# Opening of an expert loop: rows of the first tiles loaded by another engine, first turned rows kept and first gate products in another order

## The reference

```python
x = hidden_states.reshape(-1, D)                       # 4096 tokens, D = 256
scores = softmax(x @ gate_w.T)                         # E = 64 experts
topk_w, topk_idx = top_k(scores, TOP_K)                # 6 experts for each token
buf[se, pos_c] = x[st]                                 # tokens sorted by expert
g = einsum('ecd,efd->ecf', buf, w_gate)                # F = 176
u = einsum('ecd,efd->ecf', buf, w_up)
eo = einsum('ecf,edf->ecd', silu(g) * u, w_down)
y = zeros_like(x).at[st].add(eo[se, pos_c] * weights)
```

## Time and profile before

| | us |
|---|---|
| median of 3 runs | 1659.45 |
| lowest and highest | 1658.81, 1660.39 |
| the profiled execution, own time | 1659.82 |
| its span in the trace | 1658.0 |

### The profile page before, as it was taken

How to read it: one execution, slowest core, us unless ns; L and a number is a source line. 1 busy time by engine, 2 the same in 40 slices (tenths; PEclk the granted TensorE clock), 3 DMA queues, 4 the chain that set the end, 5 groups by cost and what they waited for, 6 DMA issues and landing times. The chain is left out here.

```text
span 1658.0 us, 44404 instructions
## 1 busy us (share of the span) xinstructions
PE 1496.2 (90%) x12590; PEld 1005.8 (61%) x12655; DVE 1272.3 (77%) x4402; ACT 1003.2 (61%) x2284; POOL 786.5 (47%) x848
## 2 busy tenths in 40 slices
PE   7995889999999999999974499999999999997997
PEld 4664667677777777777763255555555555554775
DVE  4663777888888888889884587777777777773887
ACT  4773676767667776676661266666666666662221
POOL 1333233666666666666677334433433443442333
PEclk9996899999999999999995699999999999998999
DMA  3874454554555542223223666666666667524996
GB/s 115 258 236 154 128 156 124 158 160 150 156 160 160 159 148 89 88 82 94 92 69 108 175 183 203 195 194 199 201 192 195 205 191 204 183 79 97 251 246 144
DMA packets 264982, 264.40 MB, mean 159 GB/s; under 512 B 87467, under 2 KB 236313, under 8 KB 264752
## 3 DMA queue, kind: packets, MB, share of 16 engines
q1 hardware_dynamic: 203504, 175.70, 36.8%
q0 software_dynamic: 19968, 51.16, 8.5%
q10 hardware_dynamic: 41280, 34.77, 8.3%
HBM read 142.70 MB, written 122.98 MB: 160 GB/s over the span
## 5 line engine op out<-in xcount | busy, mean ns | idle before, releaser
L1745 POOL DMA_INDIRECT scratch_y<-e_eo,e_goes x224 | 222.6, 994 | 357.8 <-ACT e_eo L1828 314.4
L1770 PE MATMUL e_psGU<-wexp,e_xT 128*64 x896 | 290.1, 467 | 0.0
L1772 PE MATMUL e_psGU<-e_up,e_xT 128*64 128x352 f32 x896 | 290.0, 467 | 0.0
L1374 POOL TENSOR_TENSOR f_wnr<-f_wss,f_half 128x4 f32<-128x4 f32 x96 | 112.2, 1169 | 197.0 <-DVE f_wss L1197 196.9
L1364 POOL DMA_INDIRECT scratch_buf<-rows,dest x180 | 183.2, 1018 | 44.9 <-issue 43.5
L1849 ACT ACTIVATE e_up<-wexp 128x704 f32 x224 | 176.9, 790 | 20.6 <-POOLq L1735 20.6
L1770 PEld LDWEIGHTS e_psGU<-wexp,e_xT 128*64 128x64 f32 x896 | 113.8, 137 | 121.8 <-issue 121.8
L1964 DVE COPY e_down<-wexp 128x512 f32 x224 | 94.1, 420 | 101.2 <-PE e_psD L1793 99.2
L1828 ACT ACTIVATE e_eo<-e_psD 128x256 f32<-128x256 f32 x224 | 85.7, 385 | 93.7 <-PE e_psD L1793 47.0
L1817 ACT ACTIVATE e_sgm<-e_psGU 128x176 f32<-128x176 f32 x224 | 71.2, 318 | 93.3 <-PE e_psGU L1772 92.1
L1787 PE MATMUL e_psD<-wexp,e_hT 112*64 x448 | 115.2, 378 | 1.6 <-DVE e_hT L1925 1.6
(11 more groups left out here) (332 smaller groups left out, 4365.2 us busy)
## 6 DMA issues: line engine op xcount, KB each, us to landing
e_xg<-scratch_buf ACTq DMA_DIRECT2D x448, 66.0 KB
scratch_y<-f_blank SPq DMA_DIRECT2D x64, 384.0 KB
c_g<-scratch_y SPq DMA_DIRECT2D x64, 384.0 KB, 5.8
scratch_qkvT<-q_tT SPq DMA_DIRECT2D x16, 768.0 KB
wexp<-in_wgT SPq DMA_DIRECT2D x64, 176.0 KB
wexp<-in_wuT SPq DMA_DIRECT2D x64, 176.0 KB
scratch_buf<-f_blank SPq DMA_DIRECT2D x65, 132.0 KB, 1.9
scratch_kv<-q_y SPq DMA_DIRECT2D x16, 512.0 KB, 2.8
```

Of the source, the lines that this page charges most:

```text
L1374: pool.tensor_tensor(wnr[:, x, cols], wss[:, x, cols], half[:, 0:Q], ALU.pow).then_inc(wn1[x].sem, 1)
L1745: pool.indirect_dma_start(out=T["y"], out_offset=bass.IndirectOffsetOnAxis(goes[:, n:n + 1], 0), in_=eo[:, n % OB, :], in_offset=None, bou ...
L1770: pe.matmul(psGU[0:RT, n % 2, 0:2 * F], xT[:, n % 4, k, 0:RT], ring[:, bass.ds(at[n] + k * 2 * F, 2 * F)], start=(k == 0), stop=(k == KD - 1))
L1772: mm = pe.matmul(psGU[RT:P, n % 2, 0:2 * F], xT[:, n % 4, k, RT:P], up2[:, n % 2, k * 2 * F:(k + 1) * 2 * F], start=(k == 0), stop=(k == K ...
```

## The change

SyncE issues the twelve loads of tiles 2 to 7 at the start of the phase, ahead of its wait for tiles 0 and 1, and ScalarE no longer does. ScalarE makes the keeps of tiles 0 and 1 between the two first copies of up matrices, and those of tiles 2 and 3 right behind. TensorE makes the gate products of tile 0 ahead of the turns of tiles 2 and 3, and those of tile 1 behind them. From tile 2's gate products on all is as before.

```diff
--- before.py
+++ after.py
@@ -1699,6 +1699,10 @@
         @block.sync
         def _(sp):
             sp.sem_inc(ready, FIRST)
+            for m in range(2, GB, 2):
+                for i, starts in numbers(mybir.EngineType.SP, first_row, 0, E * STRETCH, m).items():
+                    for h, at in enumerate(starts):
+                        sp.dma_start(xg[i][h * RT:(h + 1) * RT, :], T["buf"][bass.ds(at, RT), :]).then_inc(gi[i], 16)
             for m in range(2):
                 sp.wait_ge(gi[m], 32)
             for ex in range(FIRST, NB):
@@ -1798,7 +1802,16 @@
                     if 0 <= m < NT:
                         stage(m)
 
-            for n in range(-4, NT + 2, 2):
+            each(turn_x, 0)
+            find(0)
+            gate_up(0)
+            each(turn_x, 2)
+            find(2)
+            gate_up(1)
+            each(turn_x, 4)
+            find(4)
+            each(turn_h, 0)
+            for n in range(2, NT + 2, 2):
                 each(gate_up, n)
                 each(down, n - 2)
                 each(down_rest, n - 2)
@@ -1854,12 +1867,12 @@
                     load_x(m, h)
             find_experts(0)
             keep_up(0)
+            keep_x(0)
+            keep_x(1)
             keep_up(1)
-            find_rows(2)
-            for m in range(2, 4):
-                for h in range(2):
-                    load_x(m, h)
-            for n in range(-4, NT + 2, 2):
+            keep_x(2)
+            keep_x(3)
+            for n in range(0, NT + 2, 2):
                 if real(n, -8):
                     find_rows(n + 8)
                 if n >= 0 and real(n, -2):
```

## The result

The changed kernel takes 1652.87 us (median of 6 runs, 1650.93 to 1655.15) beside 1659.13 us for the kernel before in the same comparison (6 runs, 1657.35 to 1660.39). The ratio is 0.9965 [0.9952, 0.9977]: 5.8 us faster, between 3.8 and 8.0; the two medians as they stand are 6.3 us apart. The direction was right and so was most of the size: the forecast had a gain of 4.3 us. Two of the later comparisons (e1 to e4, and e13 to e15) ran where every kernel, the one before too, takes about 1700 us (some 30 to 41 us more ahead of the routing stage, 3 in it, 3 in the loop); their times are set against the kernel before of the same comparison alone.

What follows compares the result with a forecast made beforehand. The prediction took TensorE to bound the experts' loop, behind an opening of waits. The profiled 1659.82 us minus 4.3 us in the opening gives 1655.5; the median lies 0.37 us lower, so 1655.2 us, range 1653.6 to 1657.4.

Steps and rivals of the forecast that it cites:

- The bound and its place: Experts' loop, 952 to 1500 us: TensorE busy 548.00 of 548.00 us; the opening ahead is a chain of waits.
- no gain at the end: Rival, chance 0.07: the loop takes the opening's gain back, through VectorE or the weights, leaving 1659.4 us.
- SyncE's weight loads: Opening: they start behind all twelve loads, near 943.5 instead of 937.97, 5.5 us later, hidden by experts loaded ahead.
- turn of tile 1: Opening, TensorE: tile 1 there at 938.7, from 937.93 plus 0.5 us for issues and 0.3 us for landing.
- second silu: Opening, ScalarE: at 944.7, 1.00 us after the first; tile 1's product, taking 1.3 us, there at 944.2.
- tile 2's products: End of the opening, TensorE: start at 945.8 instead of 950.08, a gain of 4.3 us.
- the price of two engines that issue at once: Opening: ScalarE's four loads +0.5 us beside SyncE's issues, bounds zero and 2.3 us; landing of tile 1 +0.3 us.
- The cover of VectorE: Opening: VectorE done with tile 5 at 943.6, against 944.05 for the silu; called thin, gain 1.5 us less if late.
- the keep at 943.23: Opening of the kernel before: ScalarE's first keep of turned rows, read as waiting for tile 1's turns, started at 937.93.
- The step that failed: From opening to program end: the opening's gain, 4.3 us, reaches the loop's end undiminished and the last stage starts that much sooner.
- the rivals: Two queues in each other's way (0.20), no gain at the end (0.07), slower by the clock (0.03), more than forecast (0.08).
- The range: Whole kernel: 1653.6 to 1657.4 us, for the forecast, larger gain and most of the two-queues rival, with 0.8 us scatter.

Runs made afterwards that it cites:

- e1: The kernel before, run once more without an edit: 1698.47 us beside 1699.75 us, ratio 0.9992.
- e4: The kernel before with only the order changed, all twelve loads staying on ScalarE, behind the keep of tile 1: 1702.46 us beside 1699.75, ratio 1.0006.
- e13: The changed kernel with fourteen unused turns of the identity ahead of tile 100's turn, in mid-loop: ratio 0.9978 to the kernel before.
- e15: The kernel before with fourteen unused turns of the identity ahead of tile 100's turn, in mid-loop: ratio 1.0001.
- e3: The changed kernel with the old order on TensorE and ScalarE, so only the loads move: 1695.55 us beside 1699.75, ratio 0.9975.
- e11: The changed kernel with the old order on TensorE and ScalarE, as e3, in another comparison: 1653.88 us beside 1659.13, ratio 0.9971.
- e5: The changed kernel with SyncE's twelve loads behind its wait for tiles 0 and 1: 1655.45 us beside 1658.95, ratio 0.9982.
- e6: The changed kernel with tiles 0 and 1 loaded half by half on ScalarE and SyncE: 1651.3 us, ratio 0.9960 to the kernel before.
- e8: e6 with fourteen unused turns of the identity ahead of tile 0's turn: 1651.54 us, ratio 0.9961 to the kernel before.
- e10: The changed kernel, run once more without an edit: 1654.17 us beside 1659.13 for the kernel before, ratio 0.9971.
- e2: The changed kernel, run once more without an edit: 1696.16 us beside 1699.75 for the kernel before, ratio 0.9977.
- e9: The kernel before, run once more without an edit: 1658.93 us beside 1659.13, ratio 1.0000.
- the four repeats: Unedited reruns: e1 and e9 of the kernel before (ratios 0.9992, 1.0000), e2 and e10 of the changed kernel (0.9977, 0.9971).
- e7: The changed kernel with fourteen unused turns of the identity ahead of tile 0's turn: 1652.27 us, ratio 0.9960 to the kernel before.

## Why the prediction came out as it did

**What held.** The bound and its place: the loop is full in both kernels and takes 556.4 us in both, and all that the opening gives reaches its end. The cause: ScalarE's loads ahead of its first keep (e3, e11). The rival "no gain at the end" is out. SyncE's weight loads came 4.7 us later after the first load than before and cost nothing: the loop's time and TensorE's waits in it are the same.

**The opening was mis-sized by 0.4 us**, 4.7 instead of 4.3, and by more in its single terms. Counted from the first load, forecast against measured:

| step | forecast | measured |
|---|---|---|
| turn of tile 1 | 5.3 | 4.4 |
| products of tile 0 | 6.1 | 5.3 |
| these products take | 2.4 | 2.5 |
| turns of tiles 2 and 3 take | 1.0 | 1.05 |
| first silu | 10.3 | 9.7 |
| second silu | 11.3 | 10.9 |
| tile 2's products | 12.4 | 12.0 |

The wrong term is the price of two engines that issue at once, +0.5 us for the issues and +0.3 us for the landing. It measured next to nothing on the path: 2.73 us for four issues against 2.69, a turn 0.1 us sooner than before, and in e5, without the overlap, a turn 0.07 us sooner still. I took it from an issue of 1.05 us beside SyncE's weight loads, which are another form; loads of one form side by side took 0.68 us (ScalarE) and 0.78 us (SyncE) each. The Trainium skill (Perfetto Trace Analysis, "DMA Instruction — HWDGE (DVE, Sync)") has the descriptor generator locked by one engine at a time; by that these four should have taken longer than alone, and the runs show 0.04 us of it. Of the 0.8 us gained there, 0.4 was lost again. Tile 0's products and the turns behind them took 0.2 us more than I had put, and 0.2 went to the clock between the two silus. It rose at about 941.5, so tile 1's product took 1.89 us and not 1.3, and the second silu waited 0.18 us for it; from first to second silu it was 1.20 us and not 1.00.

**The cover of VectorE was not thin.** With no price for the queues VectorE was done with tile 5 2.26 us before the silu was there, where I had 0.45 us (1.4 to 2.6 us in the other profiles with these loads and this order). The first hidden row waited for it only in e5, with SyncE's loads late, and in e6 and e8, with the first rows sooner and two more loads on SyncE. One reading of the rows was wrong without effect: the keep at 943.23 is tile 0's, and its turn had started at 936.33 already.

**The step that failed** is the one from the opening to the end of the program: "what the opening gives back reaches the end of the loop undiminished ... and the last stage starts that much sooner". I took the last stage as a fixed length. It got 1.0 us shorter, by the moment at which its clock rose; no term of the sum stood for that, and none of the rivals. The rows show it: from the stage's start to the second group of c_psG it is 4.8 us before and 3.9 after. With 4.7 instead of 4.3 and 1.0 for the last stage the sum would have been 1659.45 - 5.7 = 1653.75 us.

**The range was too narrow for what it was made of.** I allowed 0.8 us for the scatter of the runs. But the unchanged stages ahead of the opening end anywhere between 929.6 (e8) and 933.4 us (before) in the profiles at about 1655 us, and the changed kernel's median was 1652.87 in one comparison and 1654.17 in another. 1653.75 itself lies within the range; of the 0.9 us left over between it and 1652.87, 0.3 is the kernel before's own median (1659.13 beside it, 1659.45 in the forecast), and the rest is smaller than such a move. The median 1654.17 would have lain within the range, so it is in part chance that the result fell below it. Nor do the timed runs prove the last stage's part: e11 has a last stage 1.7 us longer than e10's in the profile and a median 0.3 us lower, and e3 one 1.3 us longer than e2's and a median 0.6 us lower. Between e9 and e10 the profiles have 6.0 us from the first load to the end, the medians 5.0. So what is shown is 4.7 us in the opening (the four repeats and e3, e11) and, in profiles, 1.0 us in the last stage; how much of the last microsecond of the result is the one or the other stays open.

**A version that is as good or better.** e6, the changed kernel with tiles 0 and 1 loaded by both engines, is 0.9960 [0.9946, 0.9973] of the kernel before and has the shortest way from first load to end by its profile (718.4 us, against 718.9 and 724.6), with an edit of three lines. Against the changed kernel its 1.6 us are within what a median moves.

## What to carry to other kernels

Where an engine that computes also issues DMAs, count each issue as its own work (here 0.7 us), and move those that stand ahead of the first operation that others wait for to a queue that would be waiting anyway; that alone brought here what it brought together with a new order. Take a price for contention from operations of the same form. When a gain moves the start of a stage that begins at a low clock, the stage's own length isn't fixed: allow a microsecond to either side for it.

## What the runs showed of the hardware

- Two engines issuing the same kind of load (64 rows, 66 KB) at once: 0.68 us an issue on ScalarE, 0.78 on SyncE, against 0.67 on ScalarE alone (2.69 us for four) and 0.76 on SyncE alone (9.06 us for twelve, e5). The turn of tile 0 came 3.05 to 3.27 us after the first load beside SyncE, 2.89 to 2.98 without; that of tile 1, 4.43 to 4.77 and 4.36 to 4.66.
- The last stage, same code: 141.7 to 143.4 us in seventeen profiles, with the clock's rise 2.84 to 6.21 us after its start. Fourteen turns of the identity added in the middle of the loop were enough to bring the changed kernel from 141.8 to 142.7, and the kernel before from 143.1 to 141.9.
- Work put on TensorE to raise its clock: with 2.77 us of it and a gap of 0.75 us behind, the products 3 us later were at the low clock (0.84 us for the first, e7); with the turns directly behind it they were at the high one (0.51 us, e8).
- An order that makes a few products early and then has none can keep the clock low: in e4 it stayed at 0.50 through the opening and 4.6 us into the loop, which took 2.3 us longer than in e1.
- An operation of ScalarE that stands behind loads starts when they are issued: in e4 the twelve took 9.86 us behind a keep that had to wait, and the next keep started 0.04 us after their end (992.15).
